# Attention's score tiles in two groups of four instead of three groups, and token stage and sort in one block

## The reference

```python
q, k, v = (einsum('bsm,hmd->bhsd', x, kernel[n]) for n in range(3))
attn = softmax(einsum('bhsd,bhtd->bhst', q, k) / (64 * 64 * 16))
x = layernorm(x + (attn @ v, heads joined) @ WO)
...
probs = softmax(flat @ gate_W)              # 4096 tokens, 8 experts
topk_w, topk_idx = top_k(probs, 2); topk_w /= topk_w.sum(-1)
out = 0.5 * gelu(flat @ shared_W + shared_b)
for e in range(8):
    h = gelu(flat @ W1[e] + b1[e])          # 256 -> 1024
    out += combine[:, e] * (h @ W2[e] + b2[e])
x = layernorm(x + layernorm(out) * gamma + beta)
```

## Time and profile before

| | |
|---|---|
| median of three runs (range) | 1883.01 us (1877.25 to 1883.25) |
| the profiled execution, and its span | 1879.8 us, 1878.0 us |
| busy in the span | PE 1757.6 us (94%), DVE 1385.4 (74%), ACT 1046.4 (56%), POOL 353.7 (19%) |
| attention, 180 to 500 us | PE 320.00, DVE 266.02, ACT 186.25, granted clock 1.00 |
| tokens without a stall, 1297 to 1319 us | PE 20.89, DVE 13.18, ACT 13.01, clock 1.00 |
| end of tokens and routing, 1344 to 1395 us | PE 20.36, DVE 33.72, ACT 22.17, clock 0.71 and 0.66 |
| experts, 1500 to 1700 us | PE 195.32, DVE 118.36, ACT 101.29, clock 1.00 |

### The profile page before, as it was taken

One profiled execution on the slowest core, in us unless ns is written; L12 is line 12 of the kernel. 1 busy time (PEld: TensorE's weight loads), 2 busy tenths in 40 slices (PEclk: granted clock), 3 DMA queues, 4 the chain that ended last, 5 costly groups with the idle time before them and its releaser, 6 DMA issues. The chain is left out here.

```text
span 1878.0 us, 31867 instructions
## 1 busy us (share of the span) xinstructions
PE 1757.6 (94%) x10909; PEld 1193.3 (64%) x10909; DVE 1385.4 (74%) x2213; ACT 1046.4 (56%) x1554; POOL 353.7 (19%) x399
## 2 busy tenths in 40 slices
PE   6999999999999999999999997987659999999986
PEld 5555555555555555555555553877549999999982
DVE  5888888888888888888888887555566655566647
ACT  5555555565555555555655654544455544455537
POOL 1000000000000000000000000011127766666654
PEclk9999999999999999999999998998879999999998
DMA  5011111111111111311111112444123333233335
GB/s 173 29 46 35 35 46 35 35 41 40 34 35 45 36 35 40 127 34 40 40 35 40 40 35 86 146 157 157 55 91 90 88 80 77 59 87 89 87 49 178
DMA packets 80198, 127.09 MB, mean 68 GB/s; under 512 B 12753, under 2 KB 46737, under 8 KB 77777
## 3 DMA queue, kind: packets, MB, share of 16 engines
q1 hardware_dynamic: 61808, 98.27, 15.6%
q0 software_dynamic: 18272, 27.31, 7.3%
HBM read 86.72 MB, written 38.83 MB: 67 GB/s over the span
## 5 line engine op out<-in xcount | busy, mean ns | idle before, releaser
L450 ACT ACTIVATE a_e<-banks 128x1024 f32<-128x1024 f32 x512 | 490.4, 1026 | 334.9 <-PE banks L346 334.9
L559 DVE TENSOR_TENSOR a_esum<-a_esum,a_e 128x1024 f32<-128x1024 f32 x384 | 470.4, 1225 | 80.5 <-ACT a_e L450 52.9
L360 PE MATMUL banks<-a_e,a_v 128*64 128x512 f32 x2048 | 481.6, 602 | 0.0
L360 PEld LDWEIGHTS banks<-a_e,a_v 128*64 128x64 f32 x2048 | 130.0, 136 | 251.2 <-issue 227.6
L346 PE MATMUL banks<-a_qh,a_kh 64*128 64x512 f32 x1024 | 222.8, 432 | 5.3 <-issue 5.3
L63 POOL MEMSET ident<- 128x128 f32 x1 | 0.2, 204 | 1139.9 <-POOLq L112 1139.9
L346 PEld LDWEIGHTS banks<-a_qh,a_kh 64*128 64x128 f32 x1024 | 96.2, 184 | 173.4 <-issue 107.9
L346 PE MATMUL banks<-a_qh,a_kl 64*128 64x512 f32 x1024 | 202.4, 391 | 0.0
L1790 ACT ACTIVATE e_g<-banks,e_b1c 128x256 f32<-128x256 f32 x280 | 114.9, 471 | 154.1 <-PE banks L1737 152.9
L346 PE MATMUL banks<-a_ql,a_kh 64*128 64x512 f32 x1024 | 200.2, 388 | 0.0
L1750 PE MATMUL banks<-e_w2h,e_hh 128*128 128x256 f32 x560 | 162.3, 290 | 4.5 <-issue 1.9
(11 more groups left out here) (232 smaller groups left out, 3294.4 us busy)
## 6 DMA issues: line engine op xcount, KB each, us to landing
attn_out<-a_ot SPq DMA_DIRECT2D x64, 256.0 KB, 2.0
a_inv<-inv_rows SPq DMA_DIRECT2D x126, 128.0 KB, 2.9
a_w<-w_qkv SPq DMA_DIRECT2D x32, 256.0 KB, 3.1
raw<-attn_out SPq DMA_DIRECT2D x4, 2048.0 KB, 8.8
t_ot<-attn_out SPq DMA_DIRECT2D x4, 2048.0 KB, 8.2
raw<-w_up SPq DMA_DIRECT2D x8, 1024.0 KB
raw<-w_down SPq DMA_DIRECT2D x8, 1024.0 KB
raw<-x_t SPq DMA_DIRECT2D x8, 512.0 KB, 9.3
```

The costliest lines, as they stand in the source:

```text
L360: mm = pe.matmul(o_acc[h * DH:(h + 1) * DH, :], v[quad % 2][:, n, head], e[(slot * ST + n) % NE][:, h * BANK:(h + 1) * BANK], start=n == 0 ...
L450: act.activation(e[t % NE], ring[n % RING], ACT.Exp, scale=SCALE).then_inc(e_ok, 1)
L559: dve.tensor_tensor(acc[:, :], acc[:, :], e[(slot * ST + n) % NE], ALU.add).then_inc(add_ok, 1)
```

## The change

Attention uses two groups of four tiles on the same ring of three; `e` gets NE = 8 buffers, for which several small buffers move into memory that is free by then. Tokens and routing become one block: the constants are made later, turning, `count`, `rank` and `gelu` get other steps, the parts are 8, 8, 12 and 4 tiles, the last part's ranks and totals are formed by TensorE without GpSimd's counts, the first parts' `lows` go to GpSimd, and the multiplication with the tile's number is put into `lows` (as a mark that four more steps decode behind the sort), so that `labelled` and ScalarE's part of it go. The sort's matmuls have 160 columns. The first gather is issued inside the block, and the first up weights are split behind it. The diff, cut (the semaphore names and the buffers' declarations are left out; `routing` is removed as a function and its lines stand in `tokens`, with the edits shown):

```diff
-    NE = 6
+    NE = ST
...
-        o_raw = sb("a_o_raw", [P, BANK])
-        e_turned = sb("a_e_turned", [P, S])
...
+        o_raw = wv[:, 0, :, :].rearrange("p a c -> p (a c)")
+        quarter = wv[:, 1, 0, 0:QT]
...
         RING = 3
-        GROUPS = [range(0, 3), range(3, 6), range(6, ST)]
+        GROUPS = [range(0, HALF), range(HALF, ST)]
...
             for slot in range(SLOTS):
-                for j, group in enumerate(GROUPS):
-                    for n in group:
-                        scores(slot, n)
-                    for u in units(slot) if j == 2 else ():
-                        pe_unit(pe, u)
-                    if j:
-                        for n in GROUPS[j - 1]:
-                            values(slot, n)
-                    elif slot:
-                        for n in GROUPS[-1]:
-                            values(slot - 1, n)
-            values(SLOTS - 1, ST - 2)
-            values(SLOTS - 1, ST - 1)
+                for n in GROUPS[0]:
+                    scores(slot, n)
+                for n in GROUPS[1] if slot else ():
+                    values(slot - 1, n)
+                for n in GROUPS[1]:
+                    scores(slot, n)
+                for u in units(slot):
+                    pe_unit(pe, u)
+                for n in GROUPS[0]:
+                    values(slot, n)
+            for n in GROUPS[1]:
+                values(SLOTS - 1, n)
...
+                else:
+                    act.wait_ge(wvl_ok, 2)
+                act.copy(o_raw, o_acc).then_inc(o_copied, 1)
...
-                    for u in units(slot) if j == 2 else ():
+                    for u in units(slot) if j == 1 else ():
...
-                    if slot >= 2:
-                        dve.wait_ge(turned_ok, (slot - 2) * TURNS + 1)
+                    if slot:
+                        dve.wait_ge(turned_ok, (slot - 1) * TURNS + 2)
...
-                dve.transpose(e_turned[:, :], esum[slot % 2][:, :]).then_inc(turned_ok, 1)
+                dve.transpose(esum[(slot + 1) % 2][:, :], esum[slot % 2][:, :]).then_inc(turned_ok, 1)
                 dve.wait_ge(turned_ok, n + 1)
-                dve.tensor_reduce(quarter[:, :], e_turned[:, :].rearrange("p (c k) -> p c k", k=QT), AX.X, ALU.add)\
+                dve.tensor_reduce(quarter, esum[(slot + 1) % 2][:, :].rearrange("p (c k) -> p c k", k=QT), AX.X, ALU.add)\
...
-    PARTS = [range(0, 8), range(8, 16), range(16, 24), range(24, 30), range(30, TT)]
+    PARTS = [range(0, 8), range(8, 16), range(16, TT - 4), range(TT - 4, TT)]
...
+    EARLY = {TT - 5: TT - 1}
...
+        high_hot = sb("r_high_hot", [P, CH, 2, PT], BF16)
...
-        turns = {}
-        for n in range(TT):
-            at = GROUPS[group_of[n]][-1] + LAG
-            while at in turns and at < TT:
-                at += 1
-            turns.setdefault(min(at, TT), []).append(n)
-        branch_step = {n - 1: t for t in range(TT + 1) for n in turns.get(t, []) if n}
-        branch_step[TT - 1] = TT
+        turn_at = {n: n + 5 if n < TT - 8 else TT - 3 + (n - TT + 8) // 2 for n in range(TT)}
+        last_turned = {t: [n for n in range(TT) if turn_at[n] == t] for t in range(TT + 1)}
+        branch_step = {n: EARLY.get(n, turn_at[n + 1] if n + 1 < TT else TT) for n in range(TT)}
         tops = {p: branch_step[part[-1]] for p, part in enumerate(PARTS)}
+        early_lows = TOPK * sum(len(part) for part in PARTS[:LAST - 1])
...
+            return [n for n in range(TT) if branch_step[n] + (n not in EARLY) == t]
...
+            return [n for n in EARLY if EARLY[n] == t]
...
+            sp.wait_ge(r_done, TT)
+            sp.wait_ge(pre_ok, TT)
+            sp.dma_start(b2all[:, :, :].rearrange("p e d -> p (e d)"),
+                         b2.rearrange("e d -> (e d)").partition_broadcast(P)).then_inc(bias_in, 16)
+            sp.wait_ge(plan_ok, 1)
+            first_expert = sp.value_load(plan[0:1, EXPERT, 0:1], min_val=0, max_val=E - 1)
+            for to, whole, done in ((up, w_up, up_in), (down, w_down, down_in)):
+                sp.dma_start(to[:, :], whole[bass.ds(first_expert, 1)].rearrange("a p n -> p (a n)")).then_inc(done, 16)
+            sp.wait_ge(w_t_ok, 1)
+            sp.dma_start(w_rows, w_t[:, :]).then_inc(keep["w_out"], 16)
...
+                        gp.tensor_scalar(low_hot[:, j, t, :], counting[:, :], low[:, j, t:t + 1], float(MARK + j * TT + t),
+                                         ALU.is_equal, ALU.mult).then_inc(lows_ok, 1)
...
+            gp.wait_ge(wol_ok, 2)
+            gp.memset(cum[:, 0, :], 0.0).then_inc(cum_ok, 1)
...
+                for p in range(LAST):
+                    if tops[p] + (p < LAST - 1) == t:
                         count(p)
-                while stored < len(GROUPS) and branch_step[GROUPS[stored][-1]] <= t:
+                    if p < LAST - 1 and tops[p] + 4 == t:
+                        lows(p)
...
+            gp.wait_ge(rows_out, 16 * len(GROUPS))
+            gp.wait_ge(numbers_ok, 1)
+            for a in range(CT):
+                gp.indirect_dma_start(out=xg[0][:, a, :], out_offset=None, in_=x2_rows,
+                                      in_offset=bass.IndirectOffsetOnAxis(ap=numbers[:, 0, 0, a:a + 1], axis=0))\
+                  .then_inc(xg_in[0], 16)
...
+                pe.wait_ge(hot_ok, LAST + 1)
+                start, n = PARTS[LAST][0], len(PARTS[LAST])
+                pe.matmul(ranks(LAST), before[:, :], flat(chosen, LAST), start=True, stop=False)
+                for t in range(n):
+                    mm = pe.matmul(banks[6 + LAST % 2][:, (start + t) * E:TT * E], ones[:, :],
+                                   (cum[:, start, :] if t == 0 else chosen[:, start:TT - t, :]).rearrange(
+                                       "p a b -> p (a b)") if t else
+                                   cum[:, start, :].unsqueeze(1).to_broadcast([P, n, E]), start=False, stop=t == n - 1)
+                mm.then_inc(rank_done, 1)
+            def totals():
+                pe.wait_ge(r_done, TT)
+                start = PARTS[LAST][0]
+                pe.matmul(banks[0][:, 0:E], ones[:, :], cum[:, start, :], start=True, stop=False)
+                for t in range(start, TT):
+                    mm = pe.matmul(banks[0][:, 0:E], ones[:, :], chosen[:, t, :], start=False, stop=t == TT - 1)
+                mm.then_inc(totals_ok, 1)
...
+                for n in branched_before(t):
+                    branch(n)
                 if t < TT:
                     project(t)
+                for n in branched_after(t):
+                    if turn_at[n] < t:
+                        branch(n)
+                if t == TT:
+                    rank(LAST - 1)
                 for n in turned_after(t):
                     turn(n)
-                    if n:
-                        branch(n - 1)
...
+                for n in branched_after(t):
+                    if turn_at[n] == t:
+                        branch(n)
+                for p in range(LAST - 1):
+                    if tops[p] + 3 == t:
                         rank(p)
...
+            last_rank()
+            totals()
+            pe.wait_ge(lows_ok, early_lows)
...
-                for n in turned_after(t):
+                for n in turned_after(t) if t < TT - 1 else ():
                     copy_turned(n)
-                    if n:
-                        gelu(n - 1)
+                for n in gelus_after(t):
+                    gelu(n)
+                for n in turned_after(t) if t >= TT - 1 else ():
+                    copy_turned(n)
...
+            act.wait_ge(gap_ok, 1)
+            act.activation(e2[:, :], gap[:, :], ACT.Exp).then_inc(e2_ok, 1)
+            for part in range(len(SORTS)):
+                these = SORTS[part]
+                act.wait_ge(ones_ok, part + 1)
+                act.activation(high_hot[:, these, 0, :], high_hot[:, these, 1, :], ACT.Identity, scale=own[:, :])\
+                   .then_inc(own_ok, 1)
...
-                left = logits[:, these, :]
-                for j in range(TOPK):
+                for j in steps_of:
+                    left = logits[:, these, :] if j == 0 else rest[:, 0:n, :]
...
+                    elif p < LAST:
+                        ins.then_inc(hot_ok, 1)
+                    else:
+                        link(ins)
+                        dve.tensor_tensor(chosen[:, these, :], hot[:, 0, these, :], hot[:, 1, these, :], ALU.add)\
+                           .then_inc(hot_ok, 1)
...
+                dve.wait_ge(consts_ok, 5 + E + PLANNED)
+                dve.tensor_copy(counting[:, :], counting_i[:, :])
...
+                if t and ends_group(t - 1) is not None and t < TT:
+                    inverse(ends_group(t - 1))
                 if t + 2 < TT:
                     ot_low(t + 2)
+                for n in branched_before(t):
+                    biased(n)
+                    top(LAST - 1)
                 if t < TT:
                     add(t)
                     statistics(t)
```

(45 more changed lines are left out.)

368 lines of the change are left out of this document (135 added, 233 removed).

## The result

The changed kernel takes 1823.1 us (median of 4 runs, 1819.2 to 1826.8), the kernel before 1882.9 beside it; the ratio is 0.969 (95% interval 0.9669 to 0.9711). The prediction was 1832.6 with a range of 1812 to 1858. The profiled execution after took 1826.8 (span 1825.1), so its stages can be set against those of before, whose span was 1878.0. Medians leave out disturbed executions; of the kernels tried here that is one, at 5778.9 us, of the kernel with three groups. A difference of two marks can be off by 0.1.

What follows compares the result with a forecast made beforehand. TensorE was taken to bound attention; then came its waits in the token stage and a serial tail. Savings of 14.7 + 3.3 + 23.1 + 9.3 = 50.4 from 1883.0 gave 1832.6 us, range 1812 to 1858.

Steps and rivals of the forecast that it cites:

- Attention, 14.7 forecast: Attention: two groups of four save 22.4 us, waits cost 7.7, net 14.7 us faster.
- The price per group: Attention: TensorE pays 0.35 us per score and value group opened; one fewer per slot saves 22.4 us.
- the cost of the ring's waits: Attention: with three ring tiles, each group's fourth tile waits for the first one's exponential, 7.7 us in all.
- The dear restart: Rival in attention: each fourth tile's wait costs 0.2, attention 10.9 us slower, total 1858; chance 0.16.
- the drained TensorE: Rival in attention: TensorE drains at every wait on an exponential, 81 us lost, total 1928; chance 0.04.
- The shared storage: Attention: raw output stored over used weights and transposed sums over the other sum buffer cost nothing.
- Start of the token stage: Before the token tiles: constants moved behind the first tile end VectorE's wait before splitting output weights, 3.3 us faster.
- The stream: The 32 token tiles: covered count waits and earlier normalizing and turning, 23.1 us faster, ends 8 and 37.
- the counts: Stream: later rank and count steps cover all of TensorE's 15.4 us of waits for running counts.
- the order of gelus and inverses: Stream: inverse deviation earlier, gelu a step later, saving 7.7 us, half of TensorE's 8.4 + 7.1 waits.
- The third rival: Stream finds another bound (next rows, VectorE held by GpSimd, top-2 chains): 8 instead of 23.1, total 1848; chance 0.16.
- GpSimd's comparisons: Stream: 32 small comparisons moved to GpSimd, at 0.3 us each, counted as costing nothing.

Runs made afterwards that it cites:

- the tail's parts: Changed kernel with 24 comparisons split between VectorE behind the last top-2 and GpSimd, and the up weights' split ahead of the block's end: 1823.5 us.

## Why the prediction was right, point by point

**Attention, 14.7 forecast, 12.8 measured.** The price per group and the cost of the ring's waits, both worked out from one slot of before, held: putting three groups back costs 14.5, and the two steps in the price of a slot differ by 0.127 where the waits were put at 0.12. The 12.8 is one profile against one: from the other eight profiles of the same attention it would be 13.6 to 15.8, so the 1.9 missing lie within what executions differ by. The first group's fourth tile loses 0.02 (forecast 0.03), the second group's in slots with a cast 0.15 (forecast 0.15). The dear restart fell, and so did the drained TensorE: over the whole trace the view of the score line lists a single wait of TensorE for an exponential, 0.3 us. The shared storage, which I called free, shows no cost beyond what executions differ by.

**Start of the token stage, 3.3 forecast, 3.2 measured.** The constants were the wait, and nothing took its place.

**The stream, 23.1 forecast, 28.4 measured.** The sum was near, its terms were not. I gave 15.4 to the counts and 7.7 to the order of gelus and inverses. By the runs, with the rows still late, the counts were worth 8.9 and the order 19.8. That the sum came near is luck in part. The terms failed so: I read the order's worth from TensorE's waits, the 8.4 + 7.1 of the earlier trace rows, and halved them. It was larger than even the whole of them. On ScalarE the waits for VectorE were 37.9 us before the gelus and 19.4 before the normalizing, in the view of the same stretch, and with the old order TensorE pays twice: 13.7 us more of waits for turned tiles, and passes at the lower clock behind them (mean granted clock 0.91 against 0.98), which I had left out of the term. For the counts I took the whole wait as the price, and did not ask what is late next. The third rival named it, the next half's rows, and they took 10.1 us, though they did not hold the gain down to 8.

**GpSimd's comparisons** were free as forecast, but at 0.89 each and not 0.3. That VectorE is held by GpSimd, as a way for the stream to be slower, decided nothing: without the comparisons on GpSimd it takes 139.6.

**The tail, 9.3 forecast, 8.4 measured.** Ten small matmuls more were put at 3.9 us; the two sums of 1.85 are 3.7. Wrong was that the split of the up weights would hide behind the gather and the boundary: it starts at 1339.12, behind the boundary, and keeps the rows' split 0.6 us (ScalarE's half was there at 1340.70, 1340.12 + 0.58). The larger cost, the 4.79 us of comparisons ahead of the last branches, had no step in the forecast; with half of them moved back and half on GpSimd the numbers were ready 1.7 us earlier.

**The whole.** The stages gave 52.9 against 50.4. The median gained 59.7; the other 6.8 lie in which execution was profiled: that of before was 3.1 under its median, that of after 3.7 over. The low end of the range is 1812 in the forecast; its own terms, 22.4 + 3.3 + 34 + 9.3, give 1814.

## What to carry to other kernels

Price a change of grouping on a saturated TensorE from the starts within one slot: groups opened times the restart, less the wait for the ring's tile. Here that gave 14.7 us, and 14.5 was measured, between profiles whose attention differs by up to 3.0 without an edit. A wait that TensorE shows is not what it is worth: in the stream 13.2 us of waits for the counts cost 8.9 while the next rows were late, and 12.3 us cost 16.8 once they were early. An engine two steps upstream can cost more than TensorE's own list says, so read the feeding engine's waits too, as a sign of where to look and not as a price: they had the order's two parts at 59 to 41, and these cost 70 to 30. Load by the last reader of each buffer, with a semaphore for each load: 10.1 us of the stream here for a few lines, 4.4 by the medians. And compare an edit with what the same stage does without one: the stages above differ by 2 to 12 us from profile to profile.

## What the hardware showed

- A GpSimd instruction that begins while VectorE subtracts with both inputs in SBUF is held until about the end of that subtraction: gathers' issues took 2.83 and 2.11 us instead of 1.04 and 0.96. An issue that was under way when the subtraction began was not held (1.08). In the changed kernel the same split held GpSimd's two copies of row numbers, 2.45 us beside it (1339.12 to 1341.41) against 0.31 without it, in the kernel with the tail's parts:

```profile
1339.00 2.45 POOL L1687 COPY e_numbers<-numbers 128x2 uint32<-128x2 uint32 x2 [3.00 <-POOLq L840]
```
```profile
1335.31 0.31 POOL L1691 COPY e_numbers<-numbers 128x2 uint32<-128x2 uint32 x2 [3.02 <-POOLq L840]
```

  The Trainium skill (SBUF — State Buffer, Who interferes with whom) says that a VectorE instruction with two SBUF inputs contends with one of GpSimd that reads SBUF; it takes descriptor generation to be spared by such an instruction, which it marks as inferred. The first sentence fits these rows, the second does not.
- A comparison of 128x128 against one value per partition, written as bf16, takes GpSimd 0.78 to 0.89 us (9.30 for 12, 28.1 for 32) and VectorE 0.20 (4.79 for 24).
- The same 16 sort passes took 1.27 or 2.19 us by the clock TensorE had when they came (granted 0.86 and 0.75 in the 5 us around them); with the 16 behind them that is 1.7 us in the tail, as much as most edits there are worth. Where stages are short, compare them one by one and not the whole time.
